# A deep-and-cross style tower on one Trainium2 core: layer 0 in 19 matmuls a block in place of 21, weights packed again during block 0, block 1 written out by itself

## The chip, the cores and the metric

The kernel runs on one core of one Trainium2 chip. The metric is the device time of one execution in microseconds; shorter is better. A core has five engines with queues of their own, all in order: TensorE (matmuls, in the profile PE), VectorE (DVE), ScalarE (ACT), GpSimd (POOL) and SyncE (SP), which here only starts DMAs. They meet through semaphores that the kernel sets and waits for by hand.

## What is computed

Each of 512 samples has 39 embeddings of 16 numbers, looked up by `ids` in 39 tables. Three cross layers follow, and a small perceptron:

```python
x0 = xk = e                                       # (512, 39, 16)
for W in [f0, f1, f2]:                            # (39*39,128), (128*39,128), (128*39,128)
    z = einsum('bfd,bgd->bfgd', x0, xk)           # all products of a field and a channel
    cur = einsum('bpd,pm->bmd', z, W)             # (512, 128, 16)
    outs.append(cur); xk = cur
h = concatenate([sum(concatenate(outs, 1), -1), dense_ctx], 1)
h = maximum(h @ W_top1 + b_top1, 0); h = maximum(h @ W_top2 + b_top2, 0)
y = h @ W_top3
```

In layer 0 both factors are x0, so of the 39 x 39 products only 780 differ: 39 squares and 741 pairs. Their two weights are added beforehand.

## The kernel before, in words

**Blocks.** The 512 samples go in 16 blocks of 32 samples, so 32 x 16 = 512 columns, and a block in 4 tiles of 8 samples (128 columns). TensorE runs layer 1 of block b and, in between, layer 0 of block b+1. Block 0 and the last two are written out; blocks 1 to 13 are a hardware loop (`Fori`).

**Layer 0.** SyncE writes the gathered rows of a block to a scratch in memory (`rows_to_dram`, L293), 39 rows and 20 again behind them, and reads them back shifted (`load_rows`, L310): row f of shift s is x0 of field f+s. Three shifts of 39 rows make one part of 117 partitions, so 20 shifts make 7 parts, the last of 78 rows. Loads go in three pieces (`PIECES`: parts 0 and 1 with x0t, the unshifted rows three times; parts 2 and 3; parts 4 to 6), each on semaphore `loaded[i]`. A product part (`z0`, L397, on GpSimd; `z0_of_second`, L555, on VectorE for block 1) is x0t times the loaded part. From block 2 on each part is split in two roundings so that fast matmuls keep the precision: ScalarE copies the high part z0h (`pair_high_part`, L675) and GpSimd subtracts it for the low part z0l (`pair_low_part`, L405). TensorE then does three matmuls per part, z0h with w0h, z0l with w0h, z0h with w0l (`layer0`, L849 to L851). Blocks 0 and 1 use one float32 matmul per part (L854; block 0 tile by tile, `first_tile`, L856, with the products of `z0_of_first`, L546). w0h and w0l, the two roundings of the weights, are made once, by ScalarE (L779) and VectorE (L644), before block 0.

**Between the layers.** VectorE sums the result for the output (`sum_cur0`, L569), ScalarE rounds it to x1h tile by tile (`high_part`, L685) and VectorE makes x1l (`low_part`, L563). TensorE turns x0t (`turn_x0`, L873) and ScalarE copies it as scalars x0c (`scalars`, L701). GpSimd spreads x0c to x0d (`spread`, L416).

**Layer 1.** A tile has ten groups of up to 4 fields (512 columns, the last 384), three matmuls each (L912, L913, L916). `PATTERN` says who takes a group: "a" is ScalarE, which multiplies it by the scalars into `parts` (L730, four operations), "d" is VectorE, which multiplies and adds (L606). VectorE then sums a tile in two halves (`sum_half`, L577), and TensorE multiplies the result with x0d (`grams`, L886), from which layer 2 is computed after the last block.

**Order.** Nothing is scheduled by a program: tables by (tile, group) or (tile, turn of the engine) say behind which group an engine does what else. `L0_AT` places TensorE's layer-0 parts, `TURN_AT` the turn, `ZH_AT` and `ZH_EARLY_AT` ScalarE's high parts, `SUM_AT`, `LOW_AT`, `HIGH_AT`, `SCALARS_AT` the steps between the layers; those that end in `_FIRST`, and `FIRST_AT` and its kin, hold for block 0. GpSimd's row is written out (`first_block`, L434; `block_of`, L456), gathers of rows from the tables (L388, L394) among it. After block 0 VectorE, ScalarE and TensorE have some steps between the blocks (L650, L785 to L789, L936).

psum: VectorE's groups use 2 banks in turn, ScalarE's 3, so a group waits until the one 2 or 3 before it on the same engine is done.

Of the kernel before, what the change touches and what calls it, by code (L numbers as in the profile page):

```python
# [72 lines left out]
WARMING = 4  # L73

# [11 lines left out]
SUM_AT_FIRST = (3, 2)  # L86
# [11 lines left out]
PIECE_DMAS = [2 * SPT, SPT, SPT]  # L98
# [33 lines left out]
def in_halves(b):  # L132

    return not isinstance(b, int) or b >= 2


def build(nc, tables, ids, w0a, w0b, w1, w2, wt1, bt1, wt2, bt2, wt3, dense, mask, ident, out):
# [5 lines left out]
    with ExitStack() as ctx:  # L143
# [46 lines left out]
        w1raw = graw[:, 0:F * M]  # L190
        w0braw = graw[:, F * M:F * M + L0T * M].rearrange("p (t m) -> p t m", m=M)
# [61 lines left out]
        w0l_ready = sem("w0l_ready")  # L253
        z0h_ready = sem("z0h_ready")
# [34 lines left out]
        def _(sp):  # L289
# [3 lines left out]
            def rows_to_dram(b):  # L293
# [15 lines left out]

            def load_rows(b):  # L310
                sp.wait_ge(scr_written, 16 * SCR_DMAS * b)
                for i, (first, end) in enumerate(PIECES):

                    sp.wait_ge(l0_steps, L0T * (b - 1) + end)
                    for k in range(SPT):
                        n = min(end, len(range(k, SHIFTS, SPT))) - first
                        src = bass.AP(scr_rows.tensor, (k + SPT * first) * COLS, [[COLS, F], [SPT * COLS, n], [1, COLS]])
                        sp.dma_start(pairs[F * k:F * k + F, first:first + n, :], src).then_inc(loaded[i], 16)
                    if i == 0:
# [735 lines left out]
```

## Time and profile before

| | us |
|---|---|
| three runs | 656.44, 659.19, 663.04 (median 659.19) |
| the profiled execution | 662.05 |
| its span, first to last instruction | 660.1 |
| busy: TensorE, VectorE, ScalarE, GpSimd | 629.3, 541.1, 541.4, 480.6 |
| mean granted TensorE clock | 0.984 |

The span is what the rows below are taken from; 1.95 us of the execution lie outside it. PE is the matmul side of TensorE and PEld its weight loads; busy times of matmuls overlap, since a matmul starts before the last has drained, so the distance between two starts is what one costs. "idle before <- releaser" is the time an engine stood and what ended it.

### The profile page before, as it was taken

How to read it: one execution, taken by the hardware profiler on the slowest of the kernel's cores; microseconds unless marked ns; L12 is line 12 of the kernel's file. 1: busy time of each engine (PE TensorE's matmuls, PEld its weight loads, DVE VectorE, ACT ScalarE, POOL GpSimd, SP SyncE). 2: the span in 40 equal slices, each digit the busy share in tenths (PEclk: the TensorE clock that was granted, in tenths of full speed). 3: DMA queues.
4: the chain of work that ended last, by engine and by line, in shares of the span. 5: the costliest groups of instructions: out<-in, count | busy, mean ns of one | idle time of the engine just before them, and what ended most of it. 6: DMA issues, size and time to landing. Idle time of an engine off the chain costs nothing.

```text
span 660.1 us, 12277 instructions
## 1 busy us (share of the span) xinstructions
PE 629.3 (95%) x2653; PEld 488.4 (74%) x2653; DVE 541.1 (82%) x1224; ACT 541.4 (82%) x1884; POOL 480.6 (73%) x453
## 2 busy tenths in 40 slices
PE   0879899999999999999999999999999999999898
PEld 0467588888888888888888888888888888773673
DVE  0669779898898989898989898989889898996870
ACT  1457679989898989898989898989989898994762
POOL 5888879898988989898989898989878652002330
PEclk9989999999999999999999999999999999996999
DMA  8336522313122232313132213231313303002000
GB/s 217 66 72 128 118 75 44 81 42 81 42 62 61 53 70 45 78 21 89 23 81 42 75 42 81 42 81 42 81 41 68 102 1 97 18 0 77 1 0 1
DMA packets 65502, 40.32 MB, mean 61 GB/s; under 512 B 37486, under 2 KB 50480, under 8 KB 65482
## 3 DMA queue, kind: packets, MB, share of 16 engines
q1 hardware_dynamic: 54201, 35.37, 22.2%
q0 software_dynamic: 5184, 1.29, 2.1%
q10 hardware_dynamic: 6097, 3.44, 2.1%
q8 instruction: 7, 0.11, 0.1%
q14 instruction: 13, 0.11, 0.1%
HBM read 38.13 MB, written 1.94 MB: 61 GB/s over the span
## 4 chain that ended last, share of the span: by engine, by line
PE 89%; DMA 3%; DVE 2%; issue 2%; SPq 1%; ACT 1%; POOL 1%; ACTq 0%; DVEq 0%
PE psa L916 13%; PE psa L912 13%; PE psa L913 13%; PE psd L912 8%; PE psd L916 8%; PE psd L913 8%; PE psg L886 5%; PE ps L850 4%; PE ps L849 4%; PE ps L851 3%; PE psg L976 1%; DMA x_rows_first<-emb_tiles 1%; PE psg L970 1%; PE psg L971 1%; PE psd L991 1%
## 5 line engine op out<-in xcount | busy, mean ns | idle before, releaser
L730 ACT ACTIVATE parts<-psa,x0c 128x128 f32<-128x128 f32 x1536 | 449.1, 457 | 56.4 <-PE psa L916 51.8
L606 DVE SCALAR_TENSOR_TENSOR parts<-psd,x0c,parts 128x128 f32<-128x128 f32 x960 | 265.9, 342 | 54.3 <-PE psd L916 52.4
L577 DVE TENSOR_REDUCE cur<-parts 128x64 f32<-128x1536 f32 x128 | 223.6, 1747 | 6.5 <-DVE parts L606 2.5
L912 PE MATMUL psa<-w1h,x1h 128*128 128x512 f32 x384 | 168.9, 440 | 2.0 <-ACT parts L730 1.5
L413 POOL TENSOR_TENSOR z0l<-pairs,z0h 117x512 fp32r<-117x512 f32 (+1 forms) x98 | 126.8, 1303 | 42.7 <-ACT z0h L683 42.0
L916 PE MATMUL psa<-w1h,x1l 128*128 128x512 f32 x384 | 152.4, 397 | 3.2 <-DVE x1l L567 3.2
L913 PE MATMUL psa<-w1l,x1h 128*128 128x512 f32 x384 | 151.4, 394 | 0.0
L394 POOL DMA_INDIRECT emb<-tables,idx x130 | 126.4, 972 | 24.3 <-issue 24.3
L403 POOL TENSOR_TENSOR pairs<-x0t,pairs 117x512 f32<-117x512 f32 (+1 forms) x98 | 126.7, 1302 | 3.0 <-DMA x0t<-x_rows 2.2
L912 PE MATMUL psd<-w1h,x1h 128*128 128x512 f32 (+1 forms) x256 | 100.9, 394 | 0.6 <-DVE parts L606 0.6
L916 PE MATMUL psd<-w1h,x1l 128*128 128x512 f32 (+1 forms) x256 | 97.6, 381 | 0.0
L913 PE MATMUL psd<-w1l,x1h 128*128 128x512 f32 (+1 forms) x256 | 97.4, 380 | 0.0
L912 PEld LDWEIGHTS psa<-w1h,x1h 128*128 128x128 f32 x384 | 72.4, 189 | 23.0 <-ACT parts L730 1.9
L916 PEld LDWEIGHTS psa<-w1h,x1l 128*128 128x128 f32 x384 | 72.2, 188 | 21.6 <-DVE x1l L567 3.8
L913 PEld LDWEIGHTS psa<-w1l,x1h 128*128 128x128 f32 x384 | 72.4, 189 | 20.1 <-issue 0.7
L422 POOL TENSOR_TENSOR x0d<-x0c,mask_sb 128x320 f32<-128x320 f32 x64 | 46.7, 730 | 39.7 <-PE psg L886 38.9
L683 ACT ACTIVATE z0h<-pairs 117x512 fp32r<-117x512 f32 (+1 forms) x98 | 72.1, 737 | 0.0
L912 PEld LDWEIGHTS psd<-w1h,x1h 128*128 128x128 f32 x256 | 48.1, 188 | 16.1 <-DVE parts L606 5.8
L913 PEld LDWEIGHTS psd<-w1l,x1h 128*128 128x128 f32 x256 | 48.2, 188 | 10.7 <-issue 0.7
L916 PEld LDWEIGHTS psd<-w1h,x1l 128*128 128x128 f32 x256 | 48.3, 189 | 8.8
L886 PE MATMUL psg<-x0d,cur 128*128 128x320 f32 x128 | 45.2, 435 | 0.0
L850 PE MATMUL ps<-z0l,w0h 117*128 117x512 f32 (+1 forms) x98 | 39.2, 400 | 0.0
(91 smaller groups left out, 574.3 us busy)
## 6 DMA issues: line engine op xcount, KB each, us to landing
pairs<-x_rows SPq DMA_DIRECT2D x105, 156.0 KB
pairs<-x_rows SPq DMA_DIRECT2D x30, 234.0 KB
x0t<-x_rows SPq DMA_DIRECT2D x45, 78.0 KB
gram<-w ACTq DMA_DIRECT2D x3, 832.0 KB, 7.7
emb<-tables,idx POOLq DMA_INDIRECT x130
pairs<-x_rows_first SPq DMA_DIRECT2D x8, 136.5 KB
x_rows<-emb SPq DMA_DIRECT2D x13, 72.0 KB, 2.2
wt_sb<-w_top SPq DMA_DIRECT2D x1, 768.0 KB, 6.1
```

The lines of the kernel that those rows point to most:

```text
L394: pool.indirect_dma_start(emb[0:n, c, :], None, tables, bass.IndirectOffsetOnAxis(idx[0:n, c:c + 1], 0)).then_inc(gathered, 16)
L403: pool.tensor_tensor(pairs[0:rows, k, :], x0t[0:rows, :], pairs[0:rows, k, :], ALU.mult).then_inc(z0_ready, 1)
L413: pool.tensor_tensor(low_slot(i), pairs[0:rows_of(k), k, :], high_slot(i).bitcast(F32), ALU.subtract).then_inc(z0l_ready, 1)
L577: return dve.tensor_reduce(cur1[:, t % 2, first:end], terms[:, first:end, :, :], AX.XY, ALU.add)
L606: op = dve.scalar_tensor_tensor(acc, y[:, M * j:M * j + M], x0c[:, t, GF * g + j:GF * g + j + 1], acc, ALU.mult, ALU.add)
L683: act.activation(high_slot(i), pairs[0:rows_of(k), k, :], ACT.Copy).then_inc(z0h_ready, 1)
L730: op = act.activation(lanes(dst, j), y[:, M * j:M * j + M], ACT.Copy, scale=x0c[:, t, GF * g + j:GF * g + j + 1])
L850: pe.matmul(ps0[:, :], w0h[0:rows_of(k), w], low_slot(i), start=False, stop=False)
L886: pe.matmul(psg[:, 0:TB * FX], cur1[:, t % 2, :], x0d[:, t % 2, :, :].rearrange("p b f -> p (b f)"), start=True, stop=True).then_inc(g2_do ...
L912: pe.matmul(y[:, 0:n], hi, w1h[:, c], start=True, stop=False)
L913: pe.matmul(y[:, 0:n], hi, w1l[:, c], start=False, stop=False)
L916: pe.matmul(y[:, 0:n], lo, w1h[:, c], start=False, stop=True).then_inc(full, 1)
```

## The change

1. *Packing.* Each of parts 0 to 5 becomes 128 rows: its three shifts of 39, and 11 rows more (`ROWS` to 128), loaded with an offset of their own (`XOFF`). What two of the shifts (7 and 10) would hold twice is read from other places (`MOVED`), so that shift 19, 39 products, is all that is left for part 6.
2. *Part 6* (`MIXED`) holds these 39 products three times. ScalarE makes its high part on 117 rows, GpSimd overwrites the first 39 rows with the low part (`mixed_low_part`), and the weights of the part are the sum's rounding w0h twice and w0l once (`w0_mix`), so one matmul does what took three. From block 2 on a block has 6 x 3 + 1 = 19 matmuls of layer 0. Blocks 0 and 1 keep their 7 float32 parts of 117 rows and their weights.
3. *Loads.* A block from 2 on has 18 loads in place of 12; the load of parts 2 and 3 has pieces of 29, 7 and 3 rows.
4. *Weights.* Two more inputs, `w0pa` and `w0pb`, are loaded by SyncE behind block 0's loads into `wt1_sb`; GpSimd adds them in its block-0 row, ScalarE copies w0h in tile 2 of block 0, GpSimd subtracts for w0l. The old w0h and w0l steps before block 0 are gone.
5. *Block 1* is written out on all engines but GpSimd and SyncE, with tables of its own (`SECOND_...`): the x1h, x1l and z0h steps that stood between block 0 and block 1 are inside it.
6. *Tables of block 0* are changed.

```diff
-L0_AT_FIRST = {(2, 8): [0], (3, 0): [1], (3, 2): [2], (3, 4): [3], (3, 5): [4], (3, 7): [5], (3, 8): [6]}
+L0_AT_FIRST = {(2, 7): [0], (2, 8): [1], (2, 9): [2], (3, 5): [3], (3, 6): [4, 5], (3, 7): [6]}
...
-FIRST_AT = {(0, 6): 1, (1, 0): 2, (1, 6): 3}
-FIRST_HIGH_AT = {(0, 2): 1, (1, 0): 2, (1, 3): 3}
-FIRST_Z0_AT = {(0, 0): 1, (0, 1): 2, (1, 0): 3}
-SECOND_Z0_AT = {(2, 0): [0, 1], (2, 1): [2], (2, 2): [3, 4], (2, 3): [5, 6]}
+FIRST_AT = {(0, 3): 1, (1, 0): 2, (1, 7): 3}
+FIRST_HIGH_AT = {(0, 2): 1, (1, 0): 2, (1, 2): 3}
+FIRST_Z0_AT = {(0, 0): 1, (0, 2): 2, (1, 0): 3}
+SECOND_Z0_AT = {(2, 0): [0, 1], (2, 2): [2], (2, 3): [3], (3, 0): [4], (3, 1): [5, 6]}
...
+SECOND_HIGH_AT = {(0, 0): 1, (0, 5): 2, (1, 0): 3}
+SECOND_LOW_AT = {(0, 0): 1, (0, 2): 2, (0, 3): 3}
+SECOND_ZH_AT = {(0, 3): 0, (0, 5): 1, (1, 0): 2, (1, 1): 3, (1, 2): 4, (1, 4): 5, (1, 5): 6}
+L0_AT_SECOND = {(1, 3): [0], (1, 4): [1], (1, 6): [2], (1, 9): [3], (2, 2): [4], (2, 3): [5], (2, 4): [6]}
+W0_MIX_AT = (1, 3)
+W0H_AT_FIRST = (2, 3)
...
-SUM_AT_FIRST = (3, 2)
+SUM_AT_FIRST = (3, 1)
...
-PIECE_DMAS = [2 * SPT, SPT, SPT]
+FIRST_PIECE_DMAS = [2 * SPT, SPT, SPT]
+PIECE_DMAS = [2 * SPT + 2, SPT + 3, SPT + 1]
...
+XF, XN = 10, 128 - ROWS
+XOFF = [18, 21, 29, 32]
+MOVED = {7: (3, 10, 18), 10: (0, 10, 21)}
+MIXED = L0T - 1
...
+            def load_piece(i, first, end):
+
+                for k in range(SPT):
+                    s = SPT * first + k
+                    if s in MOVED:
+                        low, high, away = MOVED[s]
+                        also, until, away2 = MOVED[s + SPT]
+                        load_some(i, k, first, 2, high, F - high, high + s, SPT)
+                        load_some(i, k, first, 2, low, high - low, low + away, away2 - away)
+                        load_some(i, k, first, 2, also, low - also, also + s, away2 - s)
+                    else:
+                        load_some(i, k, first, end - first, 0, F, s, SPT)
...
+            sp.dma_start(w0p.rearrange("p (t m) -> p t m", m=M), w0pa).then_inc(w0p_in, 16)
+            sp.dma_start(w0pb_raw.rearrange("p (t m) -> p t m", m=M), w0pb).then_inc(w0p_in, 16)
             for b in range(1, NBLK):
                 rows_to_dram(b)
                 load_rows(b)
...
-                for c in range(7):
+                for c in range(4):
+                    gather_early(1, c)
+                pool.wait_ge(w0p_in, 32)
+                pool.tensor_tensor(w0p, w0p, w0pb_raw, ALU.add).then_inc(w0p_summed, 1)
+                for c in range(4, 7):
                     gather_early(1, c)
                 spread(0, 3)
                 gather_early(1, 7)
+                pool.wait_ge(w0h_ready, 1)
+                pool.tensor_tensor(w0l[:, :], w0p, w0h[:, :].bitcast(F32), ALU.subtract).then_inc(w0l_ready, 1)
...
+                        if starts(b) and (t, n) == W0H_AT_FIRST:
+                            act.wait_ge(w0p_summed, 1)
+                            act.activation(w0h[:, :], w0p, ACT.Copy).then_inc(w0h_ready, 1)
...
+                    if k == MIXED:
+
+                        pe.matmul(ps0[:, :], w0l[0:ROWS, w], high_slot(i), start=False, stop=True).then_inc(l0_steps, 1)
+                        return
```

ScalarE in tile 2 of block 0, before: its groups are `parts`, the copies of scalars `x0c`.

```order
L730 ACTIVATE parts<-psa,x0c 128x128 x16
L713 ACTIVATE gram<-psg 128x40x8
L730 ACTIVATE parts<-psa,x0c 128x128 x4
L709 ACTIVATE x0c<-pst 128x39
L730 ACTIVATE parts<-psa,x0c 128x128 x4
L709 ACTIVATE x0c<-pst 128x39
```

The same place in the changed kernel:

```order
L817 ACTIVATE parts<-psa,x0c 128x128 x20
L800 ACTIVATE gram<-psg 128x40x8
L817 ACTIVATE parts<-psa,x0c 128x128 x8
L830 ACTIVATE w0h<-wt_sb 128x896
L817 ACTIVATE parts<-psa,x0c 128x128 x8
L789 ACTIVATE x0c<-pst 128x39
```

The copy w0h now stands between the tile's fourth and fifth group, and the scalars behind the sixth. On GpSimd, from the spread of tile 2 of block 0 to the first products of block 2, before:

```order
L422 TENSOR_TENSOR x0d<-x0c,mask_sb 128x320
L388 DMA emb_first<-tables,idx_first 128x16 x7
L422 TENSOR_TENSOR x0d<-x0c,mask_sb 128x320
L388 DMA emb_first<-tables,idx_first 128x16
L403 TENSOR_TENSOR pairs<-x0t,pairs 117x512
L388 DMA emb_first<-tables,idx_first 128x16
```

and in the changed kernel:

```order
L498 TENSOR_TENSOR x0d<-x0c,mask_sb 128x320
L458 DMA emb_first<-tables,idx_first 128x16 x4
L521 TENSOR_TENSOR wt_sb<-wt_sb 128x896
L458 DMA emb_first<-tables,idx_first 128x16 x3
L498 TENSOR_TENSOR x0d<-x0c,mask_sb 128x320
L458 DMA emb_first<-tables,idx_first 128x16
L527 TENSOR_TENSOR w0l<-wt_sb,w0h 128x896
L473 TENSOR_TENSOR pairs<-x0t,pairs 128x512
```

Two operations of 896 columns are new, one behind the fourth gather, one ahead of the first product. On SyncE, the loads of block 2, before:

```order
L318 DMA pairs<-x_rows 39x2x512 x3
L327 DMA x0t<-x_rows 39x512 x3
L318 DMA pairs<-x_rows 39x2x512 x3
L318 DMA pairs<-x_rows 39x3x512 x2
L318 DMA pairs<-x_rows 39x2x512
```

and in the changed kernel:

```order
L348 DMA pairs<-x_rows 39x2x512 x3
L365 DMA pairs<-x_rows 11x2x512
L391 DMA x0t<-x_rows 39x512 x3
L393 DMA x0t<-x_rows 11x512
L348 DMA pairs<-x_rows 39x2x512
L348 DMA pairs<-x_rows 29x2x512
L348 DMA pairs<-x_rows 7x2x512
L348 DMA pairs<-x_rows 3x2x512
L348 DMA pairs<-x_rows 39x2x512
L365 DMA pairs<-x_rows 11x2x512
L348 DMA pairs<-x_rows 39x2x512 x3
L369 DMA pairs<-x_rows 117x1x512
```

Parts 2 and 3 come in six DMAs in place of three, one of 29 rows; part 6 comes in one of 117 rows.

## Rows read from the trace of the kernel before

**Rows 1.** Stretches: us; busy PE, PEld, DVE, ACT, POOL; clock, DMA share, GB/s.

```profile
40.00:80.00 40.00, 37.64 (x158) 28.01 (x159) 32.43 (x74) 25.25 (x92) 32.48 (x30) 0.96 0.54 116
80.00:120.00 40.00, 39.70 (x167) 31.75 (x168) 34.72 (x84) 35.64 (x132) 34.95 (x34) 0.96 0.25 54
120.00:155.00 35.00, 35.00 (x155) 28.32 (x155) 31.11 (x75) 31.89 (x118) 30.96 (x30) 1.00 0.25 58
```

**Rows 2.** Waits from 120 to 560: total us, times, longest.

```profile
POOL z0l L413 <- ACT z0h L683: 38.7, 27, 5.5
```

**Rows 3.** The s-sum's register step on VectorE: ns, first and last start.

```profile
L571 DVEq FUSED_REGOPS  x13: 75/75/75, 101.6 to 519.0; - x13
```

**Rows 4.** Timeline of TensorE: start, us, what, [idle before <- releaser].

```profile
40.27 0.69 PE L916 MATMUL psa<-w1h,x1l 128*128 128x512 f32 x1 [3.16 <-DVE x1l L567]
...
40.95 3.10 PE L867 MATMUL ps<-pairs,w0s 117*128 117x128 f32 x14
...
52.68 0.64 PE L912 MATMUL psa<-w1h,x1h 128*128 128x512 f32 x1
...
74.51 0.49 PE L912 MATMUL psa<-w1h,x1h 128*128 128x512 f32 x1 [0.16 <-ACT x1h L699]
...
79.84 0.50 PE L912 MATMUL psa<-w1h,x1h 128*128 128x512 f32 x1 [1.51 <-ACT parts L730]
...
81.49 0.63 PE L913 MATMUL psd<-w1l,x1h 128*128 128x512 f32 x1
81.92 0.63 PE L916 MATMUL psd<-w1h,x1l 128*128 128x512 f32 x1
...
86.01 0.39 PE L851 MATMUL ps<-z0h,w0l 117*128 117x512 f32 x1
86.24 0.56 PE L877 MATMUL pst<-ident_sb,x0t 117*128 117x117 f32 x4
```

**Rows 5.** The chain that ended last: start, us, what.

```profile
112.93 0.54 PE psg L886 x2
```

**Rows 6.** Timeline of GpSimd: blocks 0 and 1, a steady block.

```profile
53.50 0.74 POOL L422 TENSOR_TENSOR x0d<-x0c,mask_sb 128x320 f32<-128x320 f32 x1
...
58.20 2.03 POOL L388 DMA_INDIRECT emb_first<-tables,idx_first  x1 [0.30 <-issue]
...
70.21 1.29 POOL L403 TENSOR_TENSOR pairs<-x0t,pairs 117x512 f32<-117x512 f32 x1 [2.22 <-DMA x0t<-x_rows]
...
225.26 1.28 POOL L403 TENSOR_TENSOR pairs<-x0t,pairs 78x512 f32<-78x512 f32 x1
...
279.15 1.31 POOL L403 TENSOR_TENSOR pairs<-x0t,pairs 117x512 f32<-117x512 f32 x1
```

**Rows 7.** DMAs from 127.5 to 131: packets, then one queue's share of 16 engines.

```profile
DMA packets 276, 0.48 MB, mean 137 GB/s; under 512 B 42, under 2 KB 42, under 8 KB 276
...
q1 hardware_dynamic: 273, 0.48, 52.4%
```

**Rows 8.** Timeline of SyncE: start, us of the issues.

```profile
65.94 1.15 SPq L327 DMA_DIRECT2D x0t<-x_rows  x3
...
300.79 10.62 SPq L318 DMA_DIRECT2D pairs<-x_rows  x6
```

**Rows 9.** Timeline of VectorE: the first product, products 5 and 6 of block 1.

```profile
24.35 0.96 DVE L550 TENSOR_TENSOR pairs<-pairs,x0t 117x768 f32<-117x768 f32 x1 [4.96 <-DMA pairs<-x_rows_first]
...
63.99 1.28 DVE L561 TENSOR_TENSOR pairs<-x0t,pairs 117x512 f32<-117x512 f32 x2
```

**Rows 10.** The page: GB/s in 40 slices; a group of gathers, busy and mean ns.

```profile
GB/s 217 66 72 128 118 75 44 81 42 81 42 62 61 53 70 45 78 21 89 23 81 42 75 42 81 42 81 42 81 41 68 102 1 97 18 0 77 1 0 1
...
L394 POOL DMA_INDIRECT emb<-tables,idx x130 | 126.4, 972 | 24.3 <-issue 24.3
```

**Rows 11.** Timeline of ScalarE: w0h, and the fourth group of tile 2.

```profile
16.38 0.93 ACT L779 ACTIVATE w0h<-w0s 117x896 fp32r<-117x896 f32 x1
...
58.52 1.15 ACT L730 ACTIVATE parts<-psa,x0c 128x128 f32<-128x128 f32 x4
```

More of the change, by code:

```diff
@@ L119, in rows_of, with pair_rows, loads, second @@
     return F * len(range(SPT * k, min(SPT * k + SPT, SHIFTS)))
+def pair_rows(k):
+    return 128 if k < len(XOFF) else ROWS
+def loads(i, b):
+    return 16 * (FIRST_PIECE_DMAS[i] + PIECE_DMAS[i] * (b - 1))
 def starts(b):
     return isinstance(b, int) and b == 0
+def second(b):
+    return isinstance(b, int) and b == 1
 def fresh(b):
@@ L301, in rows_to_dram @@
                 if b > 1:
-                    for done, n in zip(loaded, PIECE_DMAS):
-                        sp.wait_ge(done, 16 * n * (b - 1))
+                    for i, done in enumerate(loaded):
+                        sp.wait_ge(done, loads(i, b - 1))
                 sp.dma_start(rows_at(0, 128, CH - 1), src[:, 0:CH - 1, :]).then_inc(scr_written, 16)
@@ L314, in load_rows @@
                     sp.wait_ge(l0_steps, L0T * (b - 1) + end)
[L315 to L318, printed above, removed]
+                    if b == 1:
+                        for k in range(SPT):
+                            n = min(end, len(range(k, SHIFTS, SPT))) - first
+                            src = bass.AP(scr_rows.tensor, (k + SPT * first) * COLS, [[COLS, F], [SPT * COLS, n], [1, COLS]])
+                            sp.dma_start(pairs[F * k:F * k + F, first:first + n, :], src).then_inc(loaded[i], 16)
+                    else:
+                        load_piece(i, first, min(end, MIXED))
                     if i == 0:
@@ L400, in z0 @@
                     if k == first:
-                        pool.wait_ge(loaded[i], 16 * PIECE_DMAS[i] * b)
-                rows = F * len(range(SPT * k, min(SPT * k + SPT, SHIFTS)))
+                        pool.wait_ge(loaded[i], loads(i, b))
+                rows = pair_rows(k)
                 pool.tensor_tensor(pairs[0:rows, k, :], x0t[0:rows, :], pairs[0:rows, k, :], ALU.mult).then_inc(z0_ready, 1)
@@ L609, in block_of @@
                         op.then_inc(acc_steps, 1)
-                        if (t, n) == (0, 0) and not starts(b):
+                        if (t, n) == (0, 0) and not starts(b) and not second(b):
                             low_part(b, TILES - 1)
@@ L649, in _ @@
             block_of(0, True, slice(BB, 2 * BB))
-            low_part(1, 1)
-            low_part(1, 2)
-            with dve.Fori(1, NBLK - 2) as b:
+            block_of(1, True, slice(2 * BB, 3 * BB))
+            with dve.Fori(2, NBLK - 2) as b:
                 block_of(b, True, bass.ds((b + 1) * BB, BB))
@@ L736, in block_of @@
                             gram_out(T - 2, at)
-                        if ahead and not starts(b) and (t, n) in ZH_AT:
+                        if ahead and not starts(b) and not second(b) and (t, n) in ZH_AT:
                             pair_high_part(b + 1, ZH_AT[t, n])
@@ L935, in _ @@
             block_of(0, True)
-            pe.wait_ge(w0l_ready, 1)
-            with pe.Fori(1, NBLK - 2) as b:
+            block_of(1, True)
+            with pe.Fori(2, NBLK - 2) as b:
                 block_of(b, True)
@@ L1031, in by_tile, with packed @@
         return np.ascontiguousarray(w0[rows.reshape(-1)].reshape(L0T, ROWS, M).transpose(1, 0, 2))
+    pair_f = np.zeros((L0T, 128), np.int64)
+    pair_g = np.zeros((L0T, 128), np.int64)
+    used = np.zeros((L0T, 128), bool)
+    for p in range(L0T):
+        for r in range(ROWS):
+            f, s = r % F, SPT * p + r // F
+            g = f + (SHIFTS - 1 if p == MIXED else s)
+            if p < MIXED and s in MOVED and MOVED[s][0] <= f < MOVED[s][1]:
+                g = f + MOVED[s][2]
+            pair_f[p, r], pair_g[p, r], used[p, r] = f, g % F, True
+    for p, off in enumerate(XOFF):
+        for r in range(ROWS, 128):
+            f = XF + r - ROWS
+            g = (f + off) % F
+            known = [{a, b} for a, b in zip(pair_f[0:MIXED][used[0:MIXED]], pair_g[0:MIXED][used[0:MIXED]])]
+            pair_f[p, r], pair_g[p, r], used[p, r] = f, g, {f, g} not in known
+    pairs_used = {tuple(sorted((int(a), int(b)))) for a, b in zip(pair_f[used], pair_g[used])}
+    assert len(pairs_used) == F * (F + 1) // 2 and used.sum() == len(pairs_used) + (SPT - 1) * F
+    def packed(rows, there):
+        return np.ascontiguousarray(np.where(there[:, :, None], w0[rows], 0).transpose(1, 0, 2).astype(np.float32))
     samples = np.arange(128)[:, None] // D == np.arange(TB)[None, :]
@@ L1038 @@
         "w0_mirrored": by_tile(g_of * F + f_of),
+        "w_packed": packed(pair_f * F + pair_g, used),
+        "w_packed_mirrored": packed(pair_g * F + pair_f, used & (pair_f != pair_g)),
         "w1": arr["L0_rec_f1"],
```

88 lines of the change are left out of this document (60 added, 28 removed).

## The prediction

> Times are microseconds from the start of the span. "Block b" is the stretch in which TensorE runs the 40 layer-1 groups of samples 32b to 32b+31; beside them stand the layer-0 parts 0 to 6 of block b+1. An s-time counts from a block's first group.
>
> **What bounds the kernel now.** I read the table of stretches first: TensorE is busy 35.00 of 35.00 from 120 on, the other engines 31 to 32 [rows 1]. The table of waits for 120 to 560 names no waiting matmul at all: GpSimd waits for ScalarE, 38.7 us in some 12.6 blocks, 3 us a block [rows 2]. So the steady blocks are bound by the number of columns that TensorE streams. The register step of VectorE's s-sum runs once a block, 13 times from 101.6 to 519.0, so a block is 417.4/12 = 34.78 us [rows 3]. Matmuls of 512 columns start every 0.233 us (86.01, 86.24 [rows 4]). The count closes: 108 of 512 columns and 12 of 384 are 27.3, 21 of layer 0 4.9, four grams at 0.54 2.2, the turn 0.4: 34.8 [rows 4, 5].
>
> The start is different. TensorE waits 3.16 us at 37 for x1l of tile 1, and 1.51 at 78 in block 1. After each the granted clock is low for a while: a layer-0 tile takes 3.10 us at 41 (1.8 elsewhere), and matmuls start every 0.43 at 81.5, the 1.2 GHz level and not 2.4 [rows 4]; both stretches have 0.96 on average [rows 1]. Block 1 starts at 74.51; its turn at 86.24 is 11.7 later, where 9 groups (6.3) and parts 0 and 1 (1.4) need 7.7: 4.0 us are lost. Its last gram ends, and block 2 starts, at 113.5 [rows 5].
>
> **The change, steady blocks.** Parts 0 to 5 stand on 128 partitions and not 117, part 6 takes one matmul and not three. That is two matmuls, 0.467 us, less in each of 14 blocks (layer 0 of blocks 2 to 15; block 1 keeps its float32 parts): 6.5 us. GpSimd's operations on 78 and on 117 rows take 1.28 and 1.31 [rows 6], so 11 more rows cost between 0 and 0.02 each, 0.2 a block, inside its 3 us of waits. ScalarE has the same instructions, 31.9 busy in a block that becomes 34.3.
>
> Six more DMAs a block stand on SyncE's queue, 0.4 us each, where the queue mostly waits. But the load of parts 2 and 3 now has a piece of 29 rows of two 2 KB packets. The window of three 39-row loads holds 273 packets of this queue: 234 large ones and 39 small, 13 for each DMA [rows 7]. So 39 rows went out in 13 shares of 3 rows. 29 rows have no such division. From below, the load lands like the others, 2.5 us after its start; from above, the piece's 58 packets all go through one engine, with 18 of the other five DMAs. A packet took 0.524 x 16 x 3.5 / 273 = 0.107 us, so 76 take 8.1. I take the upper end, which equal shares give. The Trainium skill ("DMA: Bandwidth & Descriptors", section "Why a DMA increments its semaphore by 16 and not by 1") has this rule: a DMA runs on the largest number of engines up to 16 that divides the slowest dimension on both sides. By that rule 39 rows give 13, as counted here, 29 give 1; the trace of before has no such load to show it.
>
> In a steady block the load is issued at s 13.4 (300.79 in the block that starts at 113.5 + 5 x 34.78 = 287.4), starts about s 15.4, lands at s 23.5 and is wanted by GpSimd at s 26.5 (279.15, a block earlier) [rows 5, 6, 8]. So 3 us cover it, and TensorE takes the finished parts 4 to 5 us after GpSimd has them.
>
> **The change, block 0.** w0h and w0l go from 16 to 19 us: worth nothing, since the first products wait for their DMA until 24.35 [rows 9]. Tile 1's layer 0 moves from behind group 6 to behind group 3: TensorE is there at 30.4 and its products come at 32.87, 2.3 us idle. Tile 2's product moves behind x1l of tile 1, so the wait of 3.16 goes. Counted with the same durations (group 0.70, layer-0 tile 1.6, VectorE's group 1.04 and half-sum 1.67, ScalarE's group 1.01) tile 2 starts at 49.3 and not 52.68 [rows 4]; a low clock after the new gap can take 1.7 of it back.
>
> That gain is not kept, because the packed weights are now made here. SyncE loads them (0.92 MB, 4.2 us at the 217 GB/s of the page's first slice [rows 10]) ahead of block 1's rows, landed near 49. GpSimd adds them after four gathers of its row, which is not moved: spread at 53.50, the fourth gather from 58.20 to 60.23 [rows 6]. The add has 896 columns where 512 take 1.30: 2.3 us, to 62.5. ScalarE waits for it in tile 2, behind its fourth group. By my count it is there at 55.4 and copies w0h at 62.5 to 63.5 (0.93 before [rows 11]). Behind that in its queue stand two groups of tile 2, done 65.5; for them waits VectorE's half-sum (67.2), then come a group, the other half, product 4 (70.6), a group, products 5 and 6 (72.9; now product 6 is done at 65.2 [rows 9]). TensorE stands 2 us near 63 for a psum bank, then for products 4 and 5, runs part 6 to 74.8 and the last groups to 76.6. So block 1 starts at 76.6, 2.1 later than now.
>
> Block 2's x0t load waits for product 6 as well: it goes out at 73.0 (65.94 now [rows 8]) and lands about 76.4. GpSimd's first product of block 2, at 70.21 now [rows 6], moves there; w0l (2.3) fits before it.
>
> **The change, block 1.** x1h, x1l and three z0h no longer stand between the blocks, so the 4.0 us of this place go. GpSimd's chain takes their place: product 0 at 76.4, a gather, product 1, a gather, product 2 at 81.3. With the 29-row piece (issued 75.0, starting near 76, 8.1 long) product 2 starts at 84.0. Two products (86.6), three low parts (90.4), then products 4, 5, 6, low 3, 4 and 5 at 1.28, a spread 0.73, the row numbers 0.2 and two gathers at 1.14: low 5 is done at 101.3. TensorE stands 3.4 us in all for part 0, tile 0's gram and part 5, and ends the block at 101.4 + 12.9 = 114.3 (part 5 0.7, part 6 0.23, groups 4 to 9 4.0, a gram, tile 3 7.4), 0.8 later than now with its own 0.47 saved. GpSimd is then some 5 us behind its steady place, makes up its 3 us of waits in block 2 and costs TensorE 0.7 there, at part 4. Block 3 starts at 149.3; now it is 148.3.
>
> **The sum.** +1.0 for the start and 12 further blocks at -0.467, -5.6, are -4.6 us. The profiled execution took 662.05 for its span of 660.1; it would take 657.4. The median of the three runs is 659.19, 0.4% below it: 659.19 - 4.6 = 654.6 is the forecast. With the 29-row piece at its lower end it is 2.0 less, 652.6.
>
> **The rivals.** (1) *The start is won.* The gather at 58.20 takes 2.03 [rows 6] where the mean is 0.97 [rows 10], in a stretch of dense DMAs; if dense stretches stand elsewhere the add comes 1.1 earlier. If TensorE and ScalarE also reach that wait later than I count (the old ScalarE ended the group before it at 59.5 [rows 11]), it hides. Then block 1 starts at 72.5 to 74 and lasts 34.3: -5 to -6.7 at the start, 13 x 0.467 = -6.1 after it, 647. For it: every load is in time; against it: the three in-order queues above. (2) *The weights' load slows the gathers.* It keeps the DMAs dense from 41 on; three more slow gathers before 60 put the add, and all that hangs on it, 2 to 3 us later: 657. For it: the same row at 58.20; against it: the mean of 0.97, though many gathers stand beside loads. (3) *Slower: the one-engine load decides in every block.* It lands at s 15.4 plus 76 packets; past s 30.8 (GpSimd's 26.5 and 4.3 of lead used up), from 0.20 us a packet on, every block is longer. At 0.22 it lands at s 32.1, 1.3 too late in 13 blocks: 659.2 + 1.0 + 13 x (1.3 - 0.47) = 671. For it: all loads of a block share that engine; against it: the queue is idle at that time now, so packets should be quick, and 0.107 includes the waiting of 13 engines for each other.
>
> **How the numbers follow.** The forecast has 0.52, the won start 0.20, the slowed gathers 0.22, the one-engine bound 0.06. The forecast case alone is 652 to 657. Cut at 648.5, inside the won start, and at 660, above the slowed gathers with the scatter of three runs (656.4 to 663.0), the range leaves out 2 in 10. Faster by over 1%, about the least that a measurement of this kernel can tell from no change, is below 652.6: a fifth of the forecast case and nearly all of the won start, 0.31. Slower by over 1% is the last rival, 0.06; within 1% 0.63.
>
> **What would show it.** Right: a step of 34.3 us from block 3 on and no waiting matmul there; ScalarE's w0h behind a wait of 5 to 7 us that GpSimd's add ends; GpSimd's first product of block 2 near 76, its third waiting for a DMA; TensorE's waits near 63 to 73 and for z0l in block 1. Wrong: w0h without a wait (rival 1); slow gathers before 58 (rival 2); steady blocks of 34.8 or more, with waits for z0l (rival 3).

## The result, and the profile after

The changed kernel takes 666.53 us (median of 20 runs, 660.07 to 671.73) where the kernel before takes 659.0 (20 runs, 655.82 to 663.04). The ratio is 1.0089, 95% interval 1.0068 to 1.011: slower by 0.9%, where 654.6 was forecast. Ratios, here and below, leave out executions in a slow state, over 1.5% above the fastest of their kernel: four of these 20 (669.99 to 671.73), without which the changed kernel's median is 664.95.

The table of stretches of the changed kernel, columns as in [rows 1]:

```profile
40.00:80.00 40.00, 33.44 (x137) 23.28 (x136) 30.35 (x61) 20.99 (x79) 23.72 (x23) 0.96 0.49 109
80.00:120.00 40.00, 34.49 (x144) 25.68 (x143) 29.24 (x69) 30.89 (x112) 33.81 (x31) 1.00 0.35 88
120.00:155.00 35.00, 34.67 (x154) 27.82 (x153) 31.11 (x74) 31.83 (x119) 32.53 (x32) 1.00 0.29 65
155.00:560.00 405.00, 402.30 (x1762) 323.46 (x1761) 358.70 (x853) 367.59 (x1340) 344.96 (x324) 1.00 0.27 63
```

TensorE lost 4.2 and 5.2 us more in the two stretches of the start than before (37.64 and 39.70 busy there [rows 1]), and in the steady part it is no longer busy all the time: 402.3 of 405. From the table of waits from 120 to 560, the one of [rows 2] and two that were not there before:

```profile
POOL z0l L483 <- ACT z0h L763: 26.3, 13, 5.7
...
DVE cur L659 <- ACT parts L817: 5.9, 13, 1.0
PE psd L1009 <- DVE parts L688: 3.0, 13, 0.3
```

Before, no matmul waited there. Now one waits 0.2 to 0.3 us in each block, for VectorE's multiplication of a group, and VectorE's half-sum waits some 0.45 for ScalarE. The step of the s-sum [rows 3], and the first line of the page's section on the chain that ended last, of the changed kernel:

```profile
L653 DVEq FUSED_REGOPS  x12: 75/75/75, 145.5 to 527.7; - x12
```

```profile
PE 63%; ACT 18%; issue 7%; DVE 6%; DMA 3%; POOL 2%; ACTq 1%; SPq 1%; DVEq 0%; POOLq 0%
```

A block (from one s-sum to the next, the "step" below) takes 382.2/11 = 34.745 us, where 417.4/12 = 34.783 stood before and 34.32 was forecast. ScalarE has 18% of the chain; in the kernel before it had 1%, and TensorE 89%.

The start: GpSimd's timeline (answers to [rows 6]), then ScalarE's [rows 11], VectorE's [rows 9] and SyncE's [rows 8], all of the changed kernel.

```profile
59.75 2.08 POOL L521 TENSOR_TENSOR wt_sb<-wt_sb 128x896 f32<-128x896 f32 x1
...
71.18 2.15 POOL L527 TENSOR_TENSOR w0l<-wt_sb,w0h 128x896 fp32r<-128x896 f32 x1
81.06 1.30 POOL L473 TENSOR_TENSOR pairs<-x0t,pairs 128x512 f32<-128x512 f32 x1 [7.73 <-DMA x0t<-x_rows]
...
89.48 2.55 POOL L473 TENSOR_TENSOR pairs<-x0t,pairs 128x512 f32<-128x512 f32 x2 [3.56 <-DMA pairs<-x_rows]
```

```profile
61.86 0.95 ACT L830 ACTIVATE w0h<-wt_sb 128x896 fp32r<-128x896 f32 x1 [3.24 <-POOL wt_sb L521]
...
112.17 0.63 ACT L763 ACTIVATE z0h<-pairs 128x512 fp32r<-128x512 f32 x1 [4.96 <-POOL pairs L473]
```

```profile
59.77 3.22 DVE L643 TENSOR_TENSOR pairs<-x0t,pairs 117x512 f32<-117x512 f32 x2
...
75.48 1.28 DVE L643 TENSOR_TENSOR pairs<-x0t,pairs 117x512 f32<-117x512 f32 x2
```

```profile
76.78 1.14 SPq L391 DMA_DIRECT2D x0t<-x_rows  x3
```

And TensorE's waits in block 1 (answers to [rows 4, 5]):

```profile
79.96 0.70 PE L983 MATMUL psg<-x0d,cur 128*128 128x320 f32 x2
...
93.41 0.47 PE L946 MATMUL ps<-z0h,w0h 128*128 128x512 f32 x1 [1.82 <-POOL z0l L483]
...
113.98 0.47 PE L1009 MATMUL psa<-w1h,x1h 128*128 128x512 f32 x1 [1.55 <-ACT parts L817]
...
122.37 0.70 PE L983 MATMUL psg<-x0d,cur 128*128 128x320 f32 x2
```

The gram at 79.96 ends block 0 and the one at 122.37 ends block 1. Block 1 starts at 80.3 (forecast 76.6, before 74.5). The start of block 2 was taken from the chain that ended last [rows 5], and there the last gram of block 1 now stands so:

```profile
122.53 0.54 PE psg L983 x2
```

So block 2 starts at 123.1 (forecast 114.3, before 113.5).

The account from profile to profile: +9.6 at the start of block 2; the s-sum stands 0.5 us earlier within its block; 11 steps at -0.04 are -0.4; so the last s-sum stands at 527.7 and not 519.0, +8.7. From there to the end it is 136.3 us and not 141.1, because in this one execution of the kernel before the granted clock was low for a while near 600 (the digit 6 in slice 37 of the page's clock row; the other profiles of this study have 134.2 to 136.3 for that piece). So the spans differ by 3.9 only, where the medians differ by 7.5 and the ratio is worth 5.9.

### The profile page after: what moved, and what is told of

It reads as the page before. It is cut to its first block, busy times and chain, and to the rows that moved or that the text cites. A ratio compares the mean times of both kernels' runs of the same rounds, so it can differ in the third digit from the quotient of the medians.

```text
span 664.0 us, 12167 instructions
## 1 busy us (share of the span) xinstructions
PE 621.5 (94%) x2625; PEld 478.5 (72%) x2625; DVE 543.1 (82%) x1223; ACT 539.9 (81%) x1886; POOL 482.1 (73%) x455
## 3 DMA queue, kind: packets, MB, share of 16 engines
q10 hardware_dynamic: 6097, 3.44, 2.0%
## 4 chain that ended last, share of the span: by engine, by line
PE 63%; ACT 18%; issue 7%; DVE 6%; DMA 3%; POOL 2%; ACTq 1%; SPq 1%; DVEq 0%; POOLq 0%
ACT parts L817 14%; PE psa L1013 8%; PE psa L1009 8%; PE psa L1010 8%; PE psd L1009 6%; PE psd L1010 5%; PE psd L1013 5%; PE psg L983 4%; DVE parts L688 3%; PE ps L946 3%; PE ps L947 3%; PE ps L948 3%; ACT gram L800 2%; DMA pairs<-x_rows 1%; PE psg L1073 1%
## 5 line engine op out<-in xcount | busy, mean ns | idle before, releaser
L659 DVE TENSOR_REDUCE cur<-parts 128x64 f32<-128x1536 f32 x128 | 223.7, 1748 | 12.9 <-ACT parts L817 7.7
L473 POOL TENSOR_TENSOR pairs<-x0t,pairs 128x512 f32<-128x512 f32 (+1 forms) x98 | 127.1, 1306 | 13.6 <-DMA x0t<-x_rows 7.7
L483 POOL TENSOR_TENSOR z0l<-pairs,z0h 128x512 fp32r<-128x512 f32 (+1 forms) x84 | 108.9, 1305 | 27.0 <-ACT z0h L763 26.3
L763 ACT ACTIVATE z0h<-pairs 128x512 fp32r<-128x512 f32 (+1 forms) x98 | 74.1, 757 | 8.8 <-POOL pairs L473 8.8
L800 ACT ACTIVATE gram<-psg 128x320 f32 (+1 forms) x64 | 35.1, 548 | 3.0 <-PE psg L983 3.0
```

Source lines behind the costliest of these rows:

```text
L473: pool.tensor_tensor(pairs[0:rows, k, :], x0t[0:rows, :], pairs[0:rows, k, :], ALU.mult).then_inc(z0_ready, 1)
L483: pool.tensor_tensor(low_slot(i), pairs[0:pair_rows(k), k, :], high_slot(i).bitcast(F32), ALU.subtract).then_inc(z0l_ready, 1)
L659: return dve.tensor_reduce(cur1[:, t % 2, first:end], terms[:, first:end, :, :], AX.XY, ALU.add)
L763: act.activation(high_slot(i), pairs[0:pair_rows(k), k, :], ACT.Copy).then_inc(z0h_ready, 1)
L800: act.activation(gram[:, :, at], psg[:, 0:TB * FX].rearrange("p (b f) -> p f b", f=FX), ACT.Copy).then_inc(g2_copied, 1)
```

## The experiments

Where an experiment has one execution, its time tells little, since the 20 of the changed kernel alone lie between 660.07 and 671.73; what counts is its profile.

Theory A, from the prediction: steady blocks are bound by TensorE's columns. Theory B: a second chain is just as long there. ScalarE's groups of tile 2 end what VectorE's half-sum waits for; VectorE's groups of tile 3 stand behind it; TensorE's group 9 of tile 3 waits for their psum bank. One steady block of the changed kernel, on VectorE and TensorE:

```profile
324.70 1.75 DVE L659 TENSOR_REDUCE cur<-parts 128x64 f32<-128x1536 f32 x1 [0.41 <-ACT parts L817]
326.37 1.12 DVE L688 SCALAR_TENSOR_TENSOR parts<-psd,x0c,parts 128x128 f32<-128x128 f32 x4
327.40 1.74 DVE L659 TENSOR_REDUCE cur<-parts 128x64 f32<-128x1536 f32 x1
329.06 1.12 DVE L688 SCALAR_TENSOR_TENSOR parts<-psd,x0c,parts 128x128 f32<-128x128 f32 x4
```

```profile
330.24 0.44 PE L1009 MATMUL psd<-w1h,x1h 128*128 128x384 f32 x1 [0.22 <-DVE parts L688]
```

In the chain that ended last this stretch reads: ScalarE from 318.54 to 329, then VectorE's groups at 329.32, then TensorE's group at 330.24, the last of the block, and columns again until tile 2 of the next.

**1. The kernel before with two matmuls fewer** (10 executions). It leaves out two products of part 6 from block 2 on, so its sum is incomplete; everything else is as before.

```diff
-                    pe.matmul(ps0[:, :], w0h[0:rows_of(k), w], high_slot(i), start=(k == 0), stop=False)
-                    pe.matmul(ps0[:, :], w0h[0:rows_of(k), w], low_slot(i), start=False, stop=False)
+                    if k < L0_END:
+                        pe.matmul(ps0[:, :], w0h[0:rows_of(k), w], high_slot(i), start=(k == 0), stop=False)
+                        pe.matmul(ps0[:, :], w0h[0:rows_of(k), w], low_slot(i), start=False, stop=False)
```

> The kernel before, with part 6 of layer 0 in one matmul of three from block 2 on (two products are left out, so that part's sum lacks z0h*w0h and z0l*w0h): 19 matmuls a block, with none of the change's loads, weights or tables. Theory A (TensorE's columns bind, and the change's own extra work takes the gain back): a block takes 34.78 - 0.47 = 34.32 us, the end comes 6.5 us earlier. Theory B (ScalarE has no slack in tiles 2 and 3, so TensorE gets ahead there and then waits for a psum bank in tile 3, through VectorE): a block takes 34.7 to 34.78, TensorE waits 0.2 to 0.4 us a block for VectorE's parts, and the end comes about 0.5 us earlier.

657.77 us, ratio 0.9989 (0.9955 to 1.0023). The step of the s-sum and the new wait of TensorE from 120 to 560:

```profile
L571 DVEq FUSED_REGOPS  x13: 75/75/75, 104.3 to 521.8; - x13
```

```profile
PE psd L913 <- DVE parts L606: 2.7, 12, 0.2
```

The step is 417.5/12 = 34.79: two matmuls fewer are worth nothing, without any other part of the change. ScalarE has 18% of the chain here too. Theory A, with the columns as the only bound, falls.

**2. Another high part moved** (one execution).

```diff
-ZH_AT = {(0, 0): 3, (0, 4): 4, (1, 2): 5, (1, 3): 6}
-ZH_EARLY_AT = {(2, 2): 0, (2, 5): 1, (3, 5): 2}
+ZH_AT = {(0, 0): 2, (0, 1): 3, (0, 4): 4, (1, 2): 5, (1, 3): 6}
+ZH_EARLY_AT = {(2, 2): 0, (2, 5): 1}
```

> The changed kernel, with ScalarE's high part 2 taken from the last turn of tile 3 to the first turns of the next block: 0.52 us of ScalarE's work leave tiles 2 and 3. Theory B: a block takes 34.32 to 34.40 instead of 34.745, TensorE's wait for VectorE's parts in tile 3 goes, end some 5 us earlier. If the high part at the last turn comes too late in the tile to count for that wait, nothing changes at all (34.745). Theory C (the 18 loads or GpSimd's 128-row operations set the period): 34.745 stays, and GpSimd waits more for ScalarE.

664.87 us, step 34.73: no help. The high part moved here stands behind the place where ScalarE is waited for. It matters which part leaves.

**3. The high parts ahead of the half-sum moved** (10 executions).

```diff
-ZH_EARLY_AT = {(2, 2): 0, (2, 5): 1, (3, 5): 2}
+ZH_EARLY_AT = {(2, 5): 0, (3, 0): 1, (3, 5): 2}
```

> The changed kernel with one table altered: ScalarE makes the high parts 0 and 1 of the block after next one turn later each (part 0 from its turn (2,2) to (2,5), part 1 from (2,5) to (3,0)), so that 0.52 us of copies leave the stretch of ScalarE's tile 2 ahead of the half-sum. Theory B (the steady block is bound by ScalarE's groups of tile 2, for which VectorE's half-sum waits, then VectorE's groups of tile 3, then TensorE): the 0.4 us at TensorE's group 9 of tile 3 go, and the step of the s-sum falls from 34.745 to 34.32 to 34.45 us; over 13 blocks -4 to -5 us, about 661.5 to 662.5. Theory A (TensorE's columns already bound it and the two matmuls saved are worth nothing for another reason, such as the rate of matmuls on 128 partitions): the step stays at 34.74 and the time at 666.5.

```profile
L653 DVEq FUSED_REGOPS  x12: 75/75/75, 150.4 to 528.7; - x12
```

378.3/11 = 34.39: inside the interval of theory B, and of TensorE's waits for VectorE's groups from 120 to 560 none is left. The median is 660.55 (661.5 to 662.5 expected), ratio to before 0.9994 (0.9953 to 1.0036), so by the two ratios some 6 us less than the changed kernel; 13 blocks at 0.35 explain 4.6 of them. The profile is of a long execution (664.80), but experiment 8 has the same step.

**4, 5. The same move in the kernel before**, with 21 and with 19 matmuls (one execution each; experiment 5 leaves out the two products of experiment 1).

> The kernel before (21 matmuls) with ScalarE's high parts 0 and 1 one turn later. Theory B has TensorE's columns and the chain of ScalarE and VectorE within 0.05 us of each other there: with the chain made 0.4 shorter the columns alone bound the block, and the step stays at 34.76 to 34.80.

> The kernel before with its last product part in one matmul of three (two of its products are left out) and the high parts one turn later: both bounds moved. Theory B: the step falls to 34.35 to 34.42, where each of the two alone leaves 34.78; theory A (matmuls saved here are not worth their columns): 34.78.

```profile
L571 DVEq FUSED_REGOPS  x13: 75/75/75, 104.8 to 523.6; - x13
```

```profile
L571 DVEq FUSED_REGOPS  x13: 75/75/75, 105.5 to 518.9; - x13
```

34.90 and 34.45 (660.43 and 655.22 us). Each change alone gives nothing (34.79, 34.90), both together 0.33; with the high parts moved, the two matmuls are worth 0.45 of their 0.467. That is what two bounds of equal length look like. Both values lie 0.03 to 0.1 above what I had written down. The trace shows where the move costs 0.12: at one group of tile 0 in each block the weight load waits for VectorE (experiment 4, block 8):

```profile
330.17 0.19 PEld L912 LDWEIGHTS psd<-w1h,x1h 128*128 128x128 f32 x1 [0.29 <-DVE parts L606]
```

Two matmul starts there are 0.33 us apart and not 0.233. Experiments 3, 5 and 8 have the same gap (0.34), so it is a third, smaller wait, and the greater part of what their steps of 34.39 to 34.45 have above 34.32.

**6. The 29-row load in two** (one execution; shown in part, the count of the piece's loads rises by one as well).

```diff
-                        load_some(i, k, first, 2, high, F - high, high + s, SPT)
+                        load_some(i, k, first, 2, high, 26, high + s, SPT)
+                        load_some(i, k, first, 2, high + 26, F - high - 26, high + 26 + s, SPT)
```

> The changed kernel, with the 29-row load of parts 2 and 3 in two loads of 26 and 3 rows. If 29 rows go through one engine and 26 through 13: the load lands 5 to 7 us earlier, GpSimd's wait of 3.56 us for it in block 1 goes, and block 2 starts 2 to 3.5 us earlier (122.9 now). If the number of rows does not matter: nothing changes. The steady block stays 34.745.

```profile
80.64 1.30 POOL L474 TENSOR_TENSOR pairs<-x0t,pairs 128x512 f32<-128x512 f32 x1 [7.46 <-DMA x0t<-x_rows]
...
85.52 2.56 POOL L474 TENSOR_TENSOR pairs<-x0t,pairs 128x512 f32<-128x512 f32 x2
```

In the changed kernel the chain that ended last runs through that load:

```profile
81.25 8.16 DMA pairs<-x_rows
```

661.3 us. GpSimd's third product no longer waits (3.56 in the changed kernel), and starts 4.9 us after the first and not 8.4; the first s-sum comes 3.1 earlier. The slow load is real (8.16 us, 8.1 forecast), and costs 3 us once. In steady blocks it costs nothing: the step stays 34.76. The rule of the Trainium skill that the prediction cites ("DMA: Bandwidth & Descriptors", section "Why a DMA increments its semaphore by 16 and not by 1") gives 29 rows one engine and 26 rows 13; this pair of runs agrees (8.16 us for the load of 29 rows, no wait for 26 and 3), though no view counts the engines.

**7. GpSimd's add ahead of the spread** (one execution).

```diff
-                spread(0, 2)
-                for c in range(4):
-                    gather_early(1, c)
                 pool.wait_ge(w0p_in, 32)
                 pool.tensor_tensor(w0p, w0p, w0pb_raw, ALU.add).then_inc(w0p_summed, 1)
-                for c in range(4, 7):
+                spread(0, 2)
+                for c in range(7):
                     gather_early(1, c)
```

> The changed kernel, with GpSimd's add of the packed weights ahead of the spread of tile 2 instead of four gathers behind it (about 53 instead of 59.8). ScalarE's wait of 3.24 us for it goes. If VectorE's product 0 of block 1 took 2.62 instead of 0.68 us because the add ran beside it, all seven products take 0.68 here, TensorE's wait of 2.61 us for it goes, and block 1 starts 2 to 3 us earlier than 80.3. If that product was slow for its loads, it stays slow.

```profile
62.87 1.30 DVE L641 TENSOR_TENSOR pairs<-x0t,pairs 117x512 f32<-117x512 f32 x2
```

663.18 us, first s-sum 1.2 earlier. ScalarE's wait for the add is gone, and VectorE's first two products take 1.30 where they took 3.22: in the changed kernel the first of them ran beside GpSimd's add (59.75 to 61.83) and ended after it. (In experiment 6 the two again ran beside the add, and took 3.44.) Block 1 starts only 0.4 us earlier, where 2 to 3 were expected: in this profile ScalarE stood 4.24 us ahead of tile 2 in a stretch that no work ends (see experiments 11 to 14), and the products themselves came 3.1 later.

**8. The three repairs together** (10 executions): edits 3, 6 and 7.

> The changed kernel with three repairs at once: the 29-row load as 26 and 3 rows, GpSimd's add of the weights ahead of the spread of tile 2 of block 0, and the two high parts of ScalarE one turn later. By the single runs the first gave -3.1 us at the first s-sum and the second -1.2; if they are separate delays the first s-sum step stands near 141.2, if one hides the other near 142.4. Theory B gives a further -4 to -5 us from the steady blocks: 657.5 to 658.5 against 659.0 of the kernel before; without it 661.5 to 662.5.

656.15 us, ratio 0.9953 (0.9911 to 0.9996). First s-sum 139.7, step 34.40; both the s-sum and the median are some 1.4 us better than the expectation had them. In the page's section on the chain ScalarE is back at 1%:

```profile
PE 79%; DVE 2%; ACT 1%; issue 1%; POOL 0%; DVEq 0%; ACTq 0%
```

**9. VectorE's products of block 1 at their old turns** (one execution).

```diff
-SECOND_Z0_AT = {(2, 0): [0, 1], (2, 2): [2], (2, 3): [3], (3, 0): [4], (3, 1): [5, 6]}
+SECOND_Z0_AT = {(2, 0): [0, 1], (2, 1): [2], (2, 2): [3, 4], (2, 3): [5, 6]}
```

> The changed kernel with VectorE's products of block 1 at the turns of the kernel before: (2,0) 0 and 1, (2,1) 2, (2,2) 3 and 4, (2,3) 5 and 6. If the late x0t load of block 2 (issued at 76.8, which waits for VectorE's last product of block 1) is what puts block 2 late, the load goes out near 70 to 72, GpSimd's first product starts near 76 in place of 81.06, and the first s-sum step comes 3 to 5 us earlier than 145.5, with a stall of TensorE in tile 2 of block 0 of up to 2 us against it. If the last product is late because w0h delays ScalarE's groups for which VectorE's half-sum waits, the turns matter little: x0t's issue moves by less than 2 us and the first step by less than 1.5.

```profile
68.78 1.14 SPq L391 DMA_DIRECT2D x0t<-x_rows  x3
```

```profile
71.90 1.29 POOL L473 TENSOR_TENSOR pairs<-x0t,pairs 128x512 f32<-128x512 f32 x1 [0.18 <-DMA x0t<-x_rows]
...
80.70 2.56 POOL L473 TENSOR_TENSOR pairs<-x0t,pairs 128x512 f32<-128x512 f32 x2 [3.98 <-DMA pairs<-x_rows]
```

658.11 us; x0t goes out 8 us earlier, GpSimd's first product starts 9.2 earlier, the first s-sum comes at 139.4, 6.1 earlier. Step 34.745, as it should be. So the turns hold block 2's chain back, by more than either case of the expectation had. Not all of the 8 us are theirs: in this profile the add came later and stood behind the first two products,

```profile
58.93 1.28 DVE L643 TENSOR_TENSOR pairs<-x0t,pairs 117x512 f32<-117x512 f32 x2
...
61.05 2.12 POOL L521 TENSOR_TENSOR wt_sb<-wt_sb 128x896 f32<-128x896 f32 x1
```

so that up to 2 us (3.22 less 1.28) went with the overlap.

**10. All four** (10 executions).

> The three repairs and VectorE's products of block 1 at their old turns, all four together. The first s-sum step stood at 145.5 in the changed kernel, 139.7 with the three repairs, 139.4 with the old turns alone. If the two shorten different waits it comes to 134 to 137 and the time to 651 to 653 (656.15 less 3 to 5); if both only take away the same lateness of block 2's chain (x0t, GpSimd's product 0) it stays at 138 to 139 and the time at 655.

655.79 us, ratio 0.9945 (0.9917 to 0.9973): no gain over the three that can be told from none. By the medians the old turns and the three repairs take away the same lateness; by the profiles that is not shown, since this one has the first s-sum at 142.5 and a stretch of 7.89 us in block 0 that no work ends, the subject of the next four.

**11 to 14. The stretches from 42 to 56** (7, 10, 10 and 10 executions). In 13 of the 16 profiles of this study ScalarE or VectorE stands in block 0 for 2 to 9 us (one has 1.7, at 60; two have none), and the trace names no instruction or DMA that ends it ("remote"; the page calls it another core or an unknown queue). Two rows from the profile of experiment 3, whose TensorE then stands 8.35 us:

```profile
DVE parts L688 <- remote: 9.4, 1, 9.4
...
ACT x1h L779 <- remote: 5.5, 1, 5.5
```

The changed kernel has 2.3 in its profile. The kernel before had none, but its variants in experiments 1, 4 and 5 had 5.6, 3.8 and 5.3. Theory C: the 0.92 MB of weights that the change loads from 40 on cause them. Experiment 11 moves these loads to 28 in the kernel with four repairs:

```diff
             for t in range(1, TILES):
                 first_rows_to_dram(t)
                 load_first_rows(t)
+                if t == 1:
+                    sp.dma_start(w0p.rearrange("p (t m) -> p t m", m=M), w0pa).then_inc(w0p_in, 16)
+                    sp.dma_start(w0pb_raw.rearrange("p (t m) -> p t m", m=M), w0pb).then_inc(w0p_in, 16)
-            sp.dma_start(w0p.rearrange("p (t m) -> p t m", m=M), w0pa).then_inc(w0p_in, 16)
-            sp.dma_start(w0pb_raw.rearrange("p (t m) -> p t m", m=M), w0pb).then_inc(w0p_in, 16)
```

> As the kernel with all four repairs, but SyncE issues the two loads of the packed weights (0.92 MB) behind the rows of tile 1 of block 0 (about 28) and not behind those of tile 3 (40). Theory C: the dense transfers from 40 to 52 delay what the engines need there, the rows of block 1 (landed at 48.7, 53.5 and 58.3 in three profiles) and ScalarE's and VectorE's stretches of 2 to 9 us from 44 to 56 that no work in the trace ends; then these stretches go or fall under 2 us, the single times scatter less than the 10 us of the kernel with three repairs (650.5 to 660.5), and the median falls by 2 to 4 us. Rival: the stretches come from the program's own length (instructions not there yet) whatever else moves; then they stand as before and the median does not improve. The rows of tiles 2 and 3 may come up to 4 us later by the traffic at 28 to 33, which would cost TensorE as much in either case.

654.67 us, ratio 0.9945 (0.9925 to 0.9964), and no such stretch in the profile: first s-sum 135.5, span 648.4. That looked like theory C, but the ratio was the same as in experiment 10. So three more: the same edit alone in the changed kernel (12), the kernel of experiment 11 once more (13), and that kernel with extra traffic into a spare place in memory (14, shown in part):

```diff
+                if b == 1:
+                    sp.dma_start(spare[0], w0pa).then_inc(spare_in, 16)
+                    sp.dma_start(spare[1], w0pb).then_inc(spare_in, 16)
```

> The changed kernel, and of it only the place of the packed weights' loads moved, from 40 to behind the rows of tile 1 (28). In it GpSimd's add does not wait for the weights in the profile, so what moves is the traffic. Theory C (the traffic from 40 on holds up ScalarE and VectorE at 44 to 56): the median falls from 666.5 to 662 to 664 and the highest single time from 671.7 to under 667. Rival (the stretches come whatever is loaded): median 665.5 to 667.5 and a highest of 669 to 672.

> The kernel of all four repairs and the early loads once more, unchanged, beside the next one: 654 to 655.5 again, single times 650 to 659, and a stretch of 2 to 8 us at 44 to 56 that no work ends in this profile if it comes by chance (the first profile had none).

> The same kernel with 0.92 MB more of traffic put on purpose where the stretches stand: SyncE copies the packed weights to a spare place in memory right behind the writes of block 1's rows (about 43), 0.92 MB read and 0.92 MB written. Theory C: the stretches of ScalarE and VectorE at 44 to 56 get longer or come in every execution, and the median rises by 3 us or more over the run beside it. Rival: the median stays within 1.5 us of it.

667.49 us for the changed kernel with early loads (ratio 1.0126, 1.0096 to 1.0157; 666.53 without them); 656.93 for the kernel once more (0.9944; the median is above the expected 654 to 655.5, the ratio that of experiment 11) and 656.88 with the extra copy (0.9945). The second profile of the same program:

```profile
49.76 1.13 DVE L688 SCALAR_TENSOR_TENSOR parts<-psd,x0c,parts 128x128 f32<-128x128 f32 x4 [6.14 <-remote]
```

with the s-sum at

```profile
L653 DVEq FUSED_REGOPS  x12: 75/75/75, 142.8 to 521.0; - x12
```

Theory C falls: the stretch comes and goes in one and the same program, 135.5 against 142.8 for the first s-sum, and neither less nor more traffic brings a change of the median that can be told from none. What it is stays open. The Trainium skill ("Runtime: NRT & Kernel Launch", section "Instruction fetch mechanics") says that each engine's instructions are fetched by a DMA queue of its own in blocks of 16 KiB, mostly hidden. The profiles here do show instruction packets, on two queues (8 and 16 of them in the changed kernel, 7 and 13 before), but in all 16 profiles one on each queue starts between 36 and 46, with the stretch and without it, so no run here shows that it is this.

## Why the prediction was wrong

The time lies outside the range (648.5 to 660) by two errors, one in the steady blocks and one in the start.

**"So the steady blocks are bound by the number of columns that TensorE streams": this step failed**, and with it 5.1 of the 5.6 us. What held in its place was a second bound of the same length: 12 blocks at 0.04 us less, where 0.467 was forecast. The reading itself was right (35.00 of 35.00 busy, no waiting matmul, a count that closes at 34.8), but it shows one bound, and says nothing of how far behind the next one is. The chain ScalarE's tile 2, half-sum, VectorE's tile 3 was within 0.04 us of it. A hint stood in the trace of before, in the table of waits of [rows 2]:

```profile
PEld psd L912 <- DVE parts L606: 2.2, 12, 0.2
```

TensorE's weight loads waited for VectorE's groups once a block, by 0.2 us. I took engines that are busy for 31 to 32 of 35 us as having 3 to 4 us to give; what counts is the one stretch of a block in which they have none left. Experiments 1, 3, 4 and 5 show both bounds.

**The start, forecast at +0.8 for block 2, was +9.6.** The chain was the one I had laid out (add, w0h, VectorE's products, x0t, GpSimd, the 29-row load), and most links were sized too short:

- "tile 2 starts at 49.3": 51.62. ScalarE had stood 2.30 us ahead of the copy of the scalars at 47.88, in a stretch that no work ends.
- w0h was copied at 61.9 and not 62.5, behind a wait of 3.2 and not 7: right in kind, at half the size.
- "then come a group, the other half, product 4 (70.6), a group, products 5 and 6 (72.9": they were done at 76.8. Part of it is the first product beside GpSimd's add, 2.6 us where 0.68 is usual, not foreseen, for which TensorE waited 2.6. The Trainium skill ("SBUF — State Buffer", section "Who interferes with whom") states that a VectorE instruction with two inputs from SBUF and a GpSimd instruction that reads it shut each other out for a whole instruction; this trace agrees (3.22 us for two products less 0.65 for the second; in experiment 7, without the overlap, both take 0.65). The larger part are the turns: my count carried the later turns of products 2 to 6 but laid the lateness to the wait for w0h. With the old turns x0t goes out at 68.8 (experiment 9), 8 us earlier; 6 to 8 of them hang on that one table, the rest on the overlap that fell away there.
- "Block 2's x0t load [...] goes out at 73.0" became 76.78, "product 0 at 76.4" became 81.06.
- "product 2 starts at 84.0": 89.48. The mechanism was right, and is shown by experiment 6; its size was 3.6 us of wait where I had 2.7.
- "ends the block at 101.4 + 12.9 = 114.3": 123.1. Of block 1's 42.8 us, where I counted 37.7, one wait had no place in my count: ScalarE's high part for block 3 in tile 3 waits 4.96 for a GpSimd that is late (112.17), with ScalarE's groups behind it; VectorE and TensorE stand 2.5 and 1.55 behind them. A late engine is late in every queue that waits for it.

**The cover of the one-engine load in steady blocks** (3 us and 4 to 5 more) held: experiment 6 leaves the step as it was. Rival 3, the slower one, is refuted; slower came by the start, with almost nothing gained in the steady blocks against it. Rival 1 is refuted, w0h did wait. Rival 2 too: the four gathers before the add took 0.95 to 1.00.

Without these faults the kernel comes near the forecast, which is in part luck. In the one profile with four repairs that has no unexplained stretch (experiment 11) block 1 starts at 75.3 and block 2 at 112.8 (76.6 and 114.3 forecast); in experiments 10 and 13 block 2 starts at 119.8 and 120.2. The step is 34.4 in all, and the medians are 655.8, 654.7 and 656.9 (654.6 forecast): 0.55% faster than the kernel before (0.7% forecast), by three intervals that all exclude 1. Of the 0.467 us a block, 0.36 to 0.40 come in (34.783 less 34.42 to 34.38).

## What to carry to other kernels

That an engine is busy for 100% of a stretch proves one bound, and says nothing of the distance to the next. Before pricing work taken off it, follow one period on the other engines and look for the stretch where they too have no idle time, and for short waits of its weight loads; a share of 90% says little. And price every moved step of a start by all that is released behind it: here the first s-sum of the changed kernel was 9.1 us late (145.5, where the kernel before has 136.4), and putting five products back by one or two turns of VectorE, with all the new instructions left in place, took 6.1 of them away.

## What the hardware showed

- VectorE's multiplication of 117x512 from two SBUF tensors takes 0.65 us, and took 2.6 beside a GpSimd add of 2.08 (changed kernel; two took 3.44 beside the add in experiment 6, and 1.30 and 1.28 without it in experiments 7 and 9).
- One program's start varied by 7 us between two executions (first s-sum 135.5 and 142.8, experiments 11 and 13), the later one with a stretch of 6.14 us that no recorded work ends. One profile of a kernel can carry this difference; medians of many executions decide.
- With two bounds of equal length, taking work off either gave nothing (34.79 and 34.90 a block, 34.78 before), off both 0.33 us (experiments 1, 4 and 5).
- 0.92 MB more read and written at 43 (experiment 14) are not seen in the median.
